# Linear attention with 32 heads (third attention of a layered model): in each step, the first half of the key and value products stands ahead of the weighted products of the step before

## The chip, the cores and the metric

One core of one Trainium2 chip runs the whole program: four layers, each with an attention part and a feed-forward part, and a gating part in front of each. The metric is the device time of one execution in microseconds, as the median of several. Inside the core five engines run on queues of their own and meet only at semaphores: TensorE (PE in the profile, its weight loads PEld), VectorE (DVE), ScalarE (ACT), GpSimd (POOL) and SyncE (SP, which issues the transfers).

## The reference, cut to what matters

The change lies in the attention of the third layer, a linear attention: the keys and values of a head are first contracted over the positions to one 64 by 64 matrix, and the queries are multiplied with that.

```python
B, S, QD = (2, 512, 256)
H, D = (32, 64)
q = jax.nn.relu(proj(Wq))
k = jax.nn.relu(proj(Wk))
v = proj(Wv)
kv = jnp.einsum('bhsd,bhse->bhde', k, v)
qkv = jnp.einsum('bhsd,bhde->bhse', q, kv)
key_sum = k.sum(axis=2)
normalizer = jnp.einsum('bhsd,bhd->bhs', q, key_sum)
normalizer = jnp.clip(normalizer, 1e-06, None)[..., None]
out = qkv / normalizer
...
return out @ Wo + bo
```

The result is added to the running sum x of the model. The gating parts need two recurrences over time for each of eight pieces (256 features by 1024 positions, cut into pieces of 128 by 256), which do not depend on x; those of the three parts that follow are computed inside this attention, in the gaps of the other engines.

## The kernel before

`stage_l2_attn` (L1708) takes the 32 heads as 16 pairs and the 1024 positions as two sequences of 512, so 32 steps: step n handles pair n // 2 and sequence n % 2. The code counts them as j = 0 to 3 within i = 0 to 7. Below, a *period* is four steps, j = 0 to 3.

For one step TensorE computes these groups, named here by letters:

- Q(n), `queries` (L1897): 6 matmuls of 512 columns into the one bank ps_q. Operands are split in a high and a low half, so each product is three matmuls.
- K0(n) and K1(n), `keys_values` with h = 0 and 1 (L1907): 12 matmuls of 256 columns each into the halves of ps_kvp, keys and values of 256 positions each.
- C(n), `key_value` (L1916): keys times values over positions, into ps_kv. These are float32 products, which the profile lists as 8 matmuls of 130 columns.
- W(n), `weighted` (L1926): queries times that matrix, the weighted products, into ps_o; also 8 records. It waits for the copy of ps_kv to SBUF (semaphore kv_evac) and for the queries (q_evac).
- T(n), `turn` (L1934): 4 transposes into ps_t, after the division (quot_ready).
- Y0(n) and Y1(n), `output` (L1940): 3 matmuls of 512 columns each, into the one bank ps_y. Each may start only when VectorE has added what stood in ps_y before to xT (semaphore y_added).

The order of TensorE is written out by hand in `step`, and is software-pipelined over three steps: Q(n), W(n-1), K0(n), Y0(n-2), K1(n), T(n-1), Y1(n-2), C(n).

VectorE has an order by hand too. Its step n is: wait for C(n) and copy ps_kv (L1859, two copies, which let W(n) go); the low half of the turned output (L1838); wait for W(n) (semaphore o_done); normalizer, its reciprocal and the division (L1867, L1868, L1870), which let T(n) go; for j = 0 to 2 the recurrences of one gating piece, `piece_scans` (L151, L156, L158: five instructions); the add of Y0(n-1) to xT (L1852, "add 0" here), which lets Y1(n-1) go; for j = 1 to 3 the quotient of a piece, `piece_finish` (L192, L195, L198); the add of Y1(n-1) ("add 1"). VectorE's step n-1 so belongs to the W(n-1) that TensorE computes within its step n, and its add 0 is that of Y0(n-2), for which Y1(n-2) waits in the same TensorE step.

ScalarE moves queries, keys and values from PSUM to SBUF (L1808, L1812, L1813), rounds the turned output to its high half (L1827) and splits weights (L1791, L1796). GpSimd makes the low halves of the weights (L1768, L1773) and the sums of the gating pieces (L175, L177, L180). SP loads the weights of a pair into two buffers in turn.

Of the kernel before, what the change touches and what calls it, by code (L numbers as in the profile page):

```python
# [90 lines left out]
def build_program(nc, io):  # L91
# [40 lines left out]
    def need(eng, semaphore, count):  # L132

        if not isinstance(count, int) or count > 0:
            eng.wait_ge(semaphore, count)
# [86 lines left out]
    def unread_products(pe, bank, count):  # L222

        for _ in range(count):
            pe.matmul(bank, ident[:, :], fside[:, 0, 0:HALF], start=True, stop=True)  # L225
# [1482 lines left out]
    def stage_l2_attn(l):  # L1708
# [5 lines left out]
        with ExitStack() as st:  # L1714
# [27 lines left out]
            def half_of(x, h):  # L1742
                return x[:, :, h * HALF:(h + 1) * HALF]
# [6 lines left out]
            @block.sync  # L1750
            def _(sp):
                def load(p, k):
                    need(sp, s["w_lo"], p - 1)
                    sp.dma_start(wqkv[:, k, :, :].rearrange("p a b -> p (a b)"), io["l2_wqkv"][p]).then_inc(s[f"wqkv{k}"], 16)
                    need(sp, s["wo_lo"], p - 1)
                    sp.dma_start(wo[:, k, :], io["l2_wo"][p]).then_inc(s[f"wo{k}"], 16)

                for p in range(PAIRS):
                    load(p, p % 2)
# [128 lines left out]
            @block.tensor  # L1888
            def _(pe):
                products = lambda w, x: ((w[0], x[0]), (w[0], x[1]), (w[1], x[0]))  # L1890
                wqkv2, xin2, wo2, oT2 = (wqkv_hi, wqkv_lo), (xin_hi, xin_lo), (wo_hi, wo_lo), (oT_hi, oT_lo)

                def queries(n, j):
                    need(pe, s["q_evac"], n)
                    for k in range(CH):
                        for m, (w, x) in enumerate(products(wqkv2, xin2)):
                            ins = pe.matmul(ps_q[:, :], w[:, j // 2, k, 0:P], half_of(x, j % 2)[:, k, :],  # L1897
                                            start=(k + m == 0), stop=(k == CH - 1 and m == 2))
                    ins.then_inc(s["q_done"], 1)

                def keys_values(n, j, h):
                    need(pe, s["kvp_evac"], 2 * n - 1 + h)
                    for a in range(2):
                        t = j % 2 * HALF + (2 * h + a) * P
                        for k in range(CH):
                            for m, (w, x) in enumerate(products(wqkv2, xin2)):
                                ins = pe.matmul(ps_kvp[:, h, a, :], x[:, k, t:t + P], w[:, j // 2, k, P:3 * P],  # L1907
                                                start=(k + m == 0), stop=(k == CH - 1 and m == 2))
                    ins.then_inc(s["kvp_done"], 1)

                def key_value(n, j):
                    pe.wait_ge(s["kvp_evac"], 2 * n + 2)
                    need(pe, s["kv_evac"], n)
                    for b in range(2):
                        for t in range(2):
                            ins = pe.matmul(ps_kv[:, 2 * HS * b:2 * HS * (b + 1)], ks[:, j % 2, 2 * b + t, :],  # L1916
                                            vs[:, j % 2, 2 * b + t, :, :].rearrange("p r e -> p (r e)"),
                                            start=(t == 0), stop=(t == 1))
                    ins.then_inc(s["kv_done"], 1)

                def weighted(n, j):
                    pe.wait_ge(s["kv_evac"], n + 1)
                    pe.wait_ge(s["q_evac"], n + 1)
                    need(pe, s["quot_ready"], n)
                    for t in range(4):
                        ins = pe.matmul(ps_o[:, t // 2, 2 * HS * (t % 2):2 * HS * (t % 2 + 1)], qT[:, j % 2, t * P:(t + 1) * P],  # L1926
                                        kv[:, j % 2, t // 2, :], start=True, stop=True)
                    ins.then_inc(s["o_done"], 1)

                def turn(n):  # L1930
                    pe.wait_ge(s["quot_ready"], n + 1)
                    need(pe, s["t_low"], n)
                    for t in range(4):
                        ins = pe.transpose(ps_t[:, t * P:(t + 1) * P], quot[:, t, :], ident[:, :])  # L1934
                    ins.then_inc(s["t_done"], 1)

                def output(n, j, ch):
                    need(pe, s["y_added"], 2 * n + ch)
                    for m, (w, o) in enumerate(products(wo2, oT2)):
                        ins = pe.matmul(ps_y[:, :], w[:, j // 2, ch * P:(ch + 1) * P], o[:, j % 2, :],  # L1940
                                        start=(m == 0), stop=(m == 2))
                    ins.then_inc(s["y_done"], 1)

                def step(n, j, i):
                    if j % 2 == 0:
                        pe.wait_ge(s["w_lo"], 2 * i + j // 2 + 1)
                    if n < 2:
                        pe.wait_ge(s["x_lo"], n + 1)
                    queries(n, j)
                    if n >= 1:  # L1950
                        weighted(n - 1, (j + 3) % 4)
                    keys_values(n, j, 0)
                    if n >= 2:
                        k = (j + 2) % 4
                        if k % 2 == 0:
                            need(pe, s["wo_lo"], 2 * i + 1 if j >= 2 else 2 * i)
                        pe.wait_ge(s["t_low"], n - 1)
                        output(n - 2, k, 0)
                    keys_values(n, j, 1)
                    if n >= 1:  # L1960
                        turn(n - 1)
                    if n >= 2:
                        output(n - 2, (j + 2) % 4, 1)
                    key_value(n, j)

                unread_products(pe, ps_y[:, :], 5)
                for n in range(STEPS):
                    step(n, n % PER, n // PER)
                weighted(STEPS - 1, 3)
                pe.wait_ge(s["wo_lo"], PAIRS)  # L1970
                pe.wait_ge(s["t_low"], STEPS - 1)
                for ch in range(CH):
                    output(STEPS - 2, 2, ch)
                turn(STEPS - 1)
                pe.wait_ge(s["t_low"], STEPS)
                for ch in range(CH):
                    output(STEPS - 1, 3, ch)
# [337 lines left out]
```

## Time and profile before

| | |
|---|---|
| median of 3 runs | 1365.04 us (1362.86 to 1367.04) |
| the profiled execution, its own time | 1363.57 us |
| its span | 1361.8 us |
| granted TensorE clock, mean over the span | 0.974 of full |
| PE busy | 1183.8 us, 87% |
| DVE busy | 974.4 us, 72% |
| ACT busy | 611.5 us, 45% |
| POOL busy | 534.5 us, 39% |

All times below are microseconds from the start of the span. 1.77 us of the profiled execution lie outside its span. The attention of the third layer runs from about 826.6 (its first Q) to about 1114. A line of the timeline gives start, duration, engine, line of the kernel, operation, output and inputs, shapes and count; in brackets stands how long the engine was idle before it and what released it. Durations of TensorE's matmuls overlap, so what one group costs is read from the start of its first matmul to the start of the next group's first.

### The profile page before, as it was taken

To read this page: it belongs to the slowest core of one execution; us is meant where nothing else is said; L and a number is where in the kernel's file an instruction comes from. 1 tells how busy PE (TensorE), PEld (TensorE's weight loads), DVE (VectorE), ACT (ScalarE), POOL (GpSimd) and SP (SyncE) were. 2 spreads that over 40 slices of the span, in tenths; PEclk is the share of its full clock that TensorE was granted. 3 is DMA by queue.
4 is the path that set the end of the run, shared out by engine and by line. 5 is a ranking of instruction groups with operands and counts; after the bars stand their busy time and mean duration, and the time that the engine had idled before them with its cause. 6 is when DMAs were issued, how large, how long until landed. Compare 5 with 4: busy or idle time off the path is not lost. (4 is left out here: it accounts for less than half of the span.)

```text
span 1361.8 us, 16948 instructions
## 1 busy us (share of the span) xinstructions
PE 1183.8 (87%) x5900; PEld 833.1 (61%) x5900; DVE 974.4 (72%) x1977; ACT 611.5 (45%) x1423; POOL 534.5 (39%) x440
## 2 busy tenths in 40 slices
PE   0088899999988888999899988999999979399997
PEld 0045556556557766433488866888888853168876
DVE  7969878788768996963633436888888878964355
ACT  2147666666555544445154424333333326143343
POOL 4427866676512221530073323444444420306520
PEclk9999999999999999999799989999999989699999
DMA  2032122121111101400543421111111000011101
GB/s 94 12 80 55 46 55 55 48 54 25 32 33 43 44 20 39 151 0 0 199 153 146 173 75 59 32 32 32 32 32 31 5 8 32 0 48 47 47 28 62
DMA packets 31092, 73.42 MB, mean 54 GB/s; under 512 B 5362, under 2 KB 15091, under 8 KB 28192
## 3 DMA queue, kind: packets, MB, share of 16 engines
q1 hardware_dynamic: 28432, 67.44, 16.2%
q0 software_dynamic: 1536, 3.86, 0.9%
q8 instruction: 47, 0.77, 0.2%
q10 hardware_dynamic: 1040, 1.05, 0.2%
q14 instruction: 37, 0.30, 0.1%
HBM read 55.89 MB, written 6.29 MB: 46 GB/s over the span
## 5 line engine op out<-in xcount | busy, mean ns | idle before, releaser
L175 POOL TENSOR_TENSOR sums<-scans 128x512 f32<-128x512 f32 x64 | 88.1, 1377 | 308.1 <-ACT terms L169 168.4
L727 PE MATMUL ps_p<-xin,wkvq 128*128 128x512 f32 x148 | 74.2, 626 | 68.6 <-DVE xin L243 65.2
L536 ACT ACTIVATE probs<-ps_s,stats 128x256 f32<-128x256 f32 (+1 forms) x256 | 104.3, 419 | 62.1 <-DVE stats L626 60.7
L483 POOL TENSOR_TENSOR probs<-probs,stats 128x512 f32<-128x512 f32 x64 | 67.3, 1051 | 119.1 <-DVE stats L632 119.1
L195 DVE RECIPROCAL sums<-sums 128x256 f32<-128x256 f32 x64 | 112.1, 1752 | 2.0
L626 DVE CUSTOM_DVE_ANT_0 ps_s<-ps_s,mask 128x256 f32<-128x256 f32 (+1 forms) x256 | 82.8, 383 | 8.9 <-PE ps_s L751 8.7
L180 POOL TENSOR_TENSOR sums<-sums,terms 128x512 f32<-128x512 f32 x64 | 84.9, 1326 | 5.0
L727 PEld LDWEIGHTS ps_p<-xin,wkvq 128*128 128x128 f32 x148 | 26.1, 196 | 90.0 <-issue 84.7
L1907 PE MATMUL K_ps_kvp<-K_wqkv_hi,K_xin_hi 128*128 128x256 f32 x256 | 74.7, 292 | 0.0
L1812 ACT ACTIVATE K_ks<-K_ps_kvp 128x256 f32<-128x256 f32 x64 | 24.6, 385 | 109.6 <-PE K_ps_kvp L1907 109.6
L925 POOL TENSOR_TENSOR L3hid<-L3hid,L3sig 128x1024 f32<-128x1024 f32 x17 | 46.1, 2716 | 70.3 <-DVE L3hid L1051 37.8
L1907 PE MATMUL K_ps_kvp<-K_wqkv_lo,K_xin_hi 128*128 128x256 f32 x256 | 72.2, 282 | 0.0
L1907 PE MATMUL K_ps_kvp<-K_wqkv_hi,K_xin_lo 128*128 128x256 f32 x256 | 72.2, 282 | 0.0
L484 POOL TENSOR_TENSOR probs<-probs,stats 128x256 f32<-128x256 f32 x64 | 68.7, 1073 | 0.0
L777 PEld LDWEIGHTS ps_o<-probT,vtok 128*64 128x64 f32 x512 | 31.4, 136 | 52.2 <-issue 29.6
L1051 DVE TENSOR_TENSOR L3hid<-L3actg,L3ps_u 128x512 f32<-128x512 f32 x34 | 23.3, 687 | 54.4 <-ACT L3actg L973 54.4
L751 PE MATMUL ps_s<-kr,qr 64*128 64x256 f32 (+1 forms) x512 | 58.8, 349 | 3.6 <-DVE qr L596 3.4
L777 PE MATMUL ps_o<-probT,vtok 128*64 128x256 f32 (+1 forms) x512 | 55.7, 338 | 3.6 <-ACT oT L551 3.6
L1662 PE MATMUL E_ps<-E_dT,E_fc 128*128 128x256 f32 x256 | 56.6, 379 | 0.6 <-ACT E_dT L1488 0.6
L1676 PE MATMUL E_ps<-E_fc,E_hid 128*128 128x256 f32 x256 | 56.4, 379 | 0.0
L751 PEld LDWEIGHTS ps_s<-kr,qr 64*128 64x128 f32 x512 | 44.0, 186 | 19.9 <-issue 10.5
L1852 DVE TENSOR_TENSOR xT<-xT,K_ps_y 128x512 f32<-128x512 f32 x64 | 43.1, 673 | 17.9 <-PE K_ps_y L1940 17.9
(411 smaller groups left out, 3501.0 us busy)
## 6 DMA issues: line engine op xcount, KB each, us to landing
E_fc<-l_fc_dram SPq DMA_DIRECT2D x16, 1024.0 KB, 7.4
qswap<-qraw SPq DMA_DIRECT2D x60, 128.0 KB, 2.3
K_wqkv<-l_wqkv_dram SPq DMA_DIRECT2D x16, 384.0 KB, 3.2
L3wgu<-L_w_dram SPq DMA_DIRECT2D x17, 256.0 KB, 2.6
L0wgu<-L_w_dram SPq DMA_DIRECT2D x14, 256.0 KB, 2.6
L3wdn<-L_w_dram SPq DMA_DIRECT2D x17, 128.0 KB, 2.0
wkvq<-w_l0a_dram SPq DMA_DIRECT2D x4, 512.0 KB, 4.1
wo<-w_l0a_dram SPq DMA_DIRECT2D x4, 512.0 KB, 3.6
```

Source lines behind the costliest of these rows:

```text
L175: pstep.mark(pool.tensor_tensor(sums[:, k, :, :], scans[:, k, :, 0, :], scans[:, k, :, 1, :], ALU.add))
L180: pool.tensor_tensor(sums[:, k, :, :], sums[:, k, :, :], terms[:, k, :, :], ALU.add).then_inc(sums_ready, 1)
L195: dstep.mark(dve.reciprocal(den, den))
L483: pool.tensor_tensor(p1, p1, rs[:, 0:2].unsqueeze(2).to_broadcast([P, 2, T]), ALU.mult)
L484: pool.tensor_tensor(p0, p0, rs[:, 2:4].unsqueeze(2).to_broadcast([P, 2, P]), ALU.mult).then_inc(s["norm_done"], 1)
L536: ins = act.activation(dst[:, i % 2, :], src[:, i % 2, :], ACT.Exp, bias=stats[:, g % 4, 4 + i:5 + i], scale=-1.0, accum_out=stats[:, g % ...
L626: ins = dve.tensor_tensor_reduce(out=view, in0=view, in1=m, scale=-1.0, scalar=-NEG, op0=ALU.add, op1=ALU.min, accum_out=stats[:, g % 4, 4 ...
L727: ins = pe.matmul(ps[:, :], w[:, k, :], xin[:, k, h * HALF:(h + 1) * HALF], start=(k == 0), stop=(k == CH - 1))
L751: ins = pe.matmul(view[:, r, :], qr[h, (4 * c + m) % 2, b * T + tile * P:b * T + tile * P + P], kr[h, c % 2, b, 0:n], start=True, stop=True)
L777: ins = pe.matmul(o, vtok[:, c % 2, 2 * b + key, 64 * r:64 * r + 64], probT[:, g % 2, r, 0:256] if key == 0 else probT[:, g % 2, r, 256:38 ...
L1662: ins = pe.matmul(ps[:, h, i * CAP:(i + 1) * CAP], fc1[:, k, c, f:f + P], dT[:, c, e * CAP:(e + 1) * CAP], start=(c == 0), stop=(c == CH - 1))
L1907: ins = pe.matmul(ps_kvp[:, h, a, :], x[:, k, t:t + P], w[:, j // 2, k, P:3 * P], start=(k + m == 0), stop=(k == CH - 1 and m == 2))
```

## The change

In TensorE's step the call of K0(n) is moved ahead of W(n-1). Nothing is added or removed. For n = 0 nothing changes, since there is no W before it, and the W of the last step stands behind the loop in both versions.

```diff
                     if n < 2:
                         pe.wait_ge(s["x_lo"], n + 1)
                     queries(n, j)
+                    keys_values(n, j, 0)
                     if n >= 1:
                         weighted(n - 1, (j + 3) % 4)
-                    keys_values(n, j, 0)
                     if n >= 2:
```

## Rows read from the trace of the kernel before

**Rows 1.** The page's first section: busy time and share of each engine.
```profile
PE 1183.8 (87%) x5900; PEld 833.1 (61%) x5900; DVE 974.4 (72%) x1977; ACT 611.5 (45%) x1423; POOL 534.5 (39%) x440
```
**Rows 2.** Busy time of PE, PEld, DVE, ACT, POOL, granted clock, transfers in a window.
```profile
930.00:965.00 35.00, 32.99 (x228) 29.49 (x227) 29.28 (x57) 12.61 (x31) 14.92 (x13) 1.00 0.10 31
```
**Rows 3.** Waits, 827 to 1115: who waited for whom; total us, times, longest.
```profile
DVE K_norm L1867 <- PE K_ps_o L1926: 22.9, 32, 1.6
PEld K_ps_y L1940 <- DVE xT L1852: 18.5, 25, 1.6
...
PEld K_ps_o L1926 <- DVE K_kv L1859: 14.2, 16, 2.0
...
PE K_ps_o L1926 <- DVE K_kv L1859: 7.5, 16, 1.8
```
**Rows 4.** Timeline of PE, two steps with recurrences and the W's that follow.
```profile
936.08 0.48 PE L1897 MATMUL K_ps_q<-K_xin_hi,K_wqkv_hi 128*128 128x512 f32 x1
...
937.55 1.05 PE L1926 MATMUL K_ps_o<-K_kv,K_qT 128*128 128x130 f32 x8
...
938.36 0.36 PE L1907 MATMUL K_ps_kvp<-K_wqkv_hi,K_xin_hi 128*128 128x256 f32 x1
...
939.87 0.40 PE L1940 MATMUL K_ps_y<-K_oT_hi,K_wo_hi 128*128 128x512 f32 x1
...
940.57 0.28 PE L1907 MATMUL K_ps_kvp<-K_wqkv_hi,K_xin_hi 128*128 128x256 f32 x1
...
942.00 0.60 PE L1934 MATMUL K_ps_t<-ident,K_quot 128*128 128x128 f32 x4
943.01 0.50 PE L1940 MATMUL K_ps_y<-K_oT_hi,K_wo_hi 128*128 128x512 f32 x1 [0.41 <-DVE xT L1852]
...
943.80 1.06 PE L1916 MATMUL K_ps_kv<-K_vs,K_ks 128*128 128x130 f32 x8
944.62 0.48 PE L1897 MATMUL K_ps_q<-K_xin_hi,K_wqkv_hi 128*128 128x512 f32 x1
...
946.09 1.05 PE L1926 MATMUL K_ps_o<-K_kv,K_qT 128*128 128x130 f32 x8
...
955.19 1.16 PE L1926 MATMUL K_ps_o<-K_kv,K_qT 128*128 128x130 f32 x8 [0.38 <-DVE K_kv L1859]
...
964.40 1.16 PE L1926 MATMUL K_ps_o<-K_kv,K_qT 128*128 128x130 f32 x8 [0.35 <-DVE K_kv L1859]
```
**Rows 5.** Timeline of PE, the step whose W is followed by no recurrences.
```profile
929.58 1.16 PE L1926 MATMUL K_ps_o<-K_kv,K_qT 128*128 128x130 f32 x8 [0.39 <-DVE K_kv L1859]
...
934.13 0.60 PE L1934 MATMUL K_ps_t<-ident,K_quot 128*128 128x128 f32 x4
934.49 0.48 PE L1940 MATMUL K_ps_y<-K_oT_hi,K_wo_hi 128*128 128x512 f32 x1
```
**Rows 6.** Timeline of DVE: normalizer, division and add 0 of a step; copies.
```profile
938.64 0.17 DVE L1867 TENSOR_SCALAR K_norm<-K_ps_o 128x8 f32<-128x8 f32 x1 [0.78 <-PE K_ps_o L1926]
...
939.08 0.69 DVE L1870 TENSOR_TENSOR K_quot<-K_ps_o,K_norm 128x512 f32<-128x512 f32 x1
...
942.29 0.66 DVE L1852 TENSOR_TENSOR xT<-xT,K_ps_y 128x512 f32<-128x512 f32 x1
...
954.55 0.59 DVE L1859 COPY K_kv<-K_ps_kv 64x130 f32<-64x130 f32 x2
```
**Rows 7.** Timeline of PE: W of steps 0, 1, 2 and 30.
```profile
834.23 1.05 PE L1926 MATMUL K_ps_o<-K_kv,K_qT 128*128 128x130 f32 x8
...
841.29 1.05 PE L1926 MATMUL K_ps_o<-K_kv,K_qT 128*128 128x130 f32 x8
...
850.69 1.16 PE L1926 MATMUL K_ps_o<-K_kv,K_qT 128*128 128x130 f32 x8 [0.29 <-DVE K_kv L1859]
...
1094.55 1.16 PE L1926 MATMUL K_ps_o<-K_kv,K_qT 128*128 128x130 f32 x8 [0.39 <-DVE K_kv L1859]
```
**Rows 8.** Timeline of PE: two 512-column matmuls after some two us of idle.
```profile
410.54 0.47 PE L1109 MATMUL L0ps_g<-L0xin_hi,L0wgu_hi 128*128 128x512 f32 x1 [2.15 <-DVE L0hid L1051]
...
1110.37 0.79 PE L1940 MATMUL K_ps_y<-K_oT_hi,K_wo_hi 128*128 128x512 f32 x1 [2.25 <-DVE K_oT_lo L1838]
```

## The prediction, made before the changed kernel was run

> **What bounds the kernel now.** I read the page's busy shares first: TensorE leads with 87% and VectorE follows with 72% [rows 1]. Then the window of one period inside the stage: in 35 us TensorE is busy 32.99 and VectorE 29.28, at full clock [rows 2]. Two engines near their limit that hand work to each other many times in a step call for the waits and their order, not for shares. The list of waits shows two on TensorE: W for VectorE's copies of ps_kv (16 times) and Y1 for add 0 (25 times), and on VectorE one for W in all 32 steps, 22.9 us [rows 3]. The PE and PEld lines of one wait are the same wait seen by two queues, so they must not be added.
>
> The timeline then gives the loop that matters. The step beginning at Q = 936.08 goes W 937.55, K0 938.36, Y0 939.87, K1 940.57, T 942.00, Y1 943.01, C 943.80, next Q 944.62, next W 946.09 [rows 4]. Costs by differences: Q 1.47, W 0.81, K0 1.51, Y0 0.70, K1 1.43, T 0.36 (934.13 to 934.49, where Y1 does not wait [rows 5]), Y1 0.79, C 0.82. They sum to 7.89. From W to W it takes 8.54, and the difference, 0.65, is the wait of Y1: it could start at 942.36 and starts at 943.01.
>
> Who ends that wait: W starts at 937.55, VectorE's normalizer at 938.64 (+1.09), and after division and five recurrence instructions add 0 runs from 942.29 to 942.95, and Y1 starts 0.06 later [rows 4, 6]. So from W to Y1 there is a chain of 5.46 through VectorE: 1.09 + 3.65 + 0.66 + 0.06. Everything that TensorE has between W and Y1 (0.81 + 1.51 + 0.70 + 1.43 + 0.36 = 4.81) hides under it. This holds for j = 0, 1, 2, whose W is followed by recurrences. For j = 3 there are none, and Y1 does not wait: 929.58 to 937.55 is 7.97 [rows 4, 5].
>
> Two of the four intervals are longer still: 946.09 to 955.19 is 9.10 and 955.19 to 964.40 is 9.21 [rows 4]. There VectorE also has a quotient to finish before the copies (954.55 + 0.59 = 955.14 [rows 6]), and W waits for these. A period is 8.54 + 9.10 + 9.21 + 7.97 = 34.82.
>
> **The change, part by part.** Only K0 moves, from behind W to ahead of it. It issues 12 matmuls and one semaphore increment, and no transfer; it passes no queue but TensorE's.
>
> *What it removes.* With K0 between Q and W, W comes 1.43 later (K1's spacing from 940.57 to 942.00, which is K0's without the slow start behind W). The copies are done 9.05 after the W before (946.09 to 955.14), so W no longer waits. That wait costs (9.10 - 8.54) + (9.21 - 8.54) = 1.23 a period, about 10 us over eight.
>
> *What it adds.* The chain from W to Y1 is not shortened: VectorE cannot begin the normalizer before W has run, and the recurrences stand behind that in its queue, add 0 behind them. But TensorE now has only W, Y0, K1 and T between W and Y1: 0.81 + 0.78 + 1.43 + 0.36 = 3.38 (Y0 taking over the slow start behind W). So Y1 waits 5.46 - 3.38 = 2.08 where it waited 0.65. And K0 has gone into the part of the loop that nothing hides. From W to W: 5.46 + Y1 0.79 + C 0.82 + Q 1.47 + K0 1.43 = 9.97. Behind the waiting Y1 stand C, the next Q, K0 and W; for W waits VectorE, whose idle ahead of the normalizer grows. That is a closed loop, so it repeats in each step with recurrences.
>
> *The four intervals after.* j = 0: 9.97 for 8.54, +1.43. j = 1: 9.97 for 9.10, +0.87. j = 2: 9.97 for 9.21, +0.76. j = 3: VectorE has no recurrences, its add 0 follows the division (2.14 after W by 939.08 + 0.61 against 937.55, or 1.8 by Y0, whichever is later), well ahead of 3.38; so TensorE's own 7.89 holds for 7.97, -0.08. Sum: 37.80 for 34.82, +2.98 a period.
>
> *What I cost at nothing.* ScalarE takes keys and values of K0 earlier relative to W; it idles before each such copy now, and C is 6.25 behind W in the slow steps, so nobody waits. T needs the division, which ends at 2.22 after W (939.08 + 0.69), and T comes at 3.02: cover 0.8, and were it gone, T would only use up part of the wait of Y1. The low halves for Y0 follow the copies (955.14 plus about 0.7), before the new W at 9.97 after the old. GpSimd's work and SP's loads get more time, not less.
>
> *The sum.* W(0), at 834.23, comes 1.43 later, and W(1) with it. W(1) to W(2) I take as another j = 1, +0.87. From W(2) at 850.69 to W(30) at 1094.55 are seven periods (243.86 us [rows 7]), 7 x 2.98 = 20.9. Behind W(30) the loop ends: the last W has no Q and K0 ahead of it, and its chain is as before. Together 1.43 + 0.87 + 20.9 = 23.2. On the profiled execution's own time, 1363.6, that is 1386.8; on the median, which lies 1.5 above it, 1388.2. I take the middle, 1387.5.
>
> *Bounds.* The uncertain term is 5.46. For the third W it may be some 0.15 more, since that W itself took 0.1 longer (1.16 against 1.05 [rows 4]), and it may shrink as little if VectorE's work meets GpSimd's elsewhere. 0.15 in 22 loops is 3.3 us; a run moves by 2. This gives 1382 to 1393.
>
> *The clock.* Idle of TensorE grows to about 1.8 us (2.08 less the tail of T) in three steps of four. After 2.15 us of idle a 512-column matmul at 410.54 still took 0.47, full speed; after 2.25 us at the end of this stage, where other waits had come just before, one took 0.79 for 0.50 [rows 4, 8], which is the lower of the two levels, 1.2 for 2.4 GHz. So the rows allow both, and the steady stage stands at 1.00 [rows 2]. The Trainium skill, page "TensorE: Matmul & The Clock Gate", section "A second HAM failure mode: psum-queue depth-cycling", says that short idles between groups of matmuls, repeated each iteration, can be enough to make the clock swing between its levels. By that rule the change would cost more than my sum; of the trace, only the row at 1110.37 speaks for it.
>
> **The rivals.** *Slower by the clock:* if one loop of each period ran at half clock from Y1 to W, its 0.79 + 0.82 + 1.47 + 1.43 = 4.51 would double: 8 x 4.5 = 36 more, 1423.
>
> *Faster:* W's wait goes and Y1's does not grow. It would need a chain from W to Y1 of at most 5.46 - 1.43 = 4.03. Then the gain is the 10 us above: 1354. For it speaks only that W's wait stands in the list; against it that 3.65 of the chain are VectorE instructions in a fixed queue.
>
> *No change:* VectorE is the bound in all steps, and a later W only moves the wait from W to Y1, one for one: 1364. This decides if VectorE has no idle between steps. It has, 22.9 us ahead of the normalizer, so it follows W.
>
> *Half of it:* only the j = 0 loops lengthen (8 x 1.43 = 11.4), because the quotients hide the rest: 1375. It needs copies later than 9.97 behind W; they are at 9.05.
>
> **How the numbers follow.** Forecast 0.80, clock 0.07, half 0.05, faster 0.04, no change 0.04. The range 1375 to 1395 takes in the bounds, a little on both sides for a mis-sized term, and the half case: over 0.8. A measurement of this kernel tells about 0.3% from no change, 4 us. Faster 0.04, same 0.04, slower 0.92.
>
> **What would show it.** The wait of W for the copies gone from the list of waits; that of Y1 for add 0 three times as long (about 24 x 2 us, less the overlap); W to W 9.97, 9.97, 9.97, 7.89; the normalizer's wait for W grown; clock 1.00. I am wrong if add 0 comes less than 4 us after W, if W to W stays near 9.1, or if matmuls of 512 columns in the stage take 0.79.

## The result, and the profile after

The changed kernel takes 1396.42 us in the median of four runs (1391.54 to 1398.08), the kernel before 1365.29 in the same comparison: a ratio of 1.0225, with an interval of 1.0199 to 1.0251, 31 us slower. The sign was forecast, the size (23 us) was not reached, and the time lies 1.4 us above the stated range. The profiled execution of the changed kernel took 1391.54, with a span of 1389.8, 28.0 longer than before.

The page's first section and the waits of the stage, from the changed kernel:

```profile
PE 1184.6 (85%) x5900; PEld 839.1 (60%) x5900; DVE 985.1 (71%) x1977; ACT 611.0 (44%) x1423; POOL 536.0 (39%) x440
```

```profile
PEld K_ps_y L1940 <- DVE xT L1852: 50.7, 25, 2.1
DVE K_norm L1867 <- PE K_ps_o L1926: 47.9, 32, 3.4
...
PEld K_ps_o L1926 <- DVE K_kv L1859: 2.7, 1, 2.7
```

Beside [rows 3]: the wait of W for the copies is gone but for the one in the last step (16 times before, once now). The wait of Y1 for add 0 has grown from 18.5 to 50.7 us, still 25 times, and VectorE's own wait for W from 22.9 to 47.9. TensorE's work is the same as in [rows 1] within 1 us; of the 28.0 us of span 27.2 are its idle time. VectorE is busy 10.7 us longer with the same 1977 instructions; the experiments trace that to one of them.

The timeline of TensorE through one step with recurrences (start, duration, engine, line, operation, count, idle before and what ended it) shows the loop:

```profile
950.94 1.05 PE L1926 MATMUL K_ps_o<-K_kv,K_qT 128*128 128x130 f32 x8
951.75 0.48 PE L1940 MATMUL K_ps_y<-K_oT_hi,K_wo_hi 128*128 128x512 f32 x1
...
953.96 0.60 PE L1934 MATMUL K_ps_t<-ident,K_quot 128*128 128x128 f32 x4
956.39 0.50 PE L1940 MATMUL K_ps_y<-K_oT_hi,K_wo_hi 128*128 128x512 f32 x1 [1.83 <-DVE xT L1852]
...
957.18 1.06 PE L1916 MATMUL K_ps_kv<-K_vs,K_ks 128*128 128x130 f32 x8
958.00 0.48 PE L1897 MATMUL K_ps_q<-K_xin_hi,K_wqkv_hi 128*128 128x512 f32 x1
...
960.90 1.05 PE L1926 MATMUL K_ps_o<-K_kv,K_qT 128*128 128x130 f32 x8
```

W at 950.94, Y1 at 956.39: the chain is 5.45 (5.46 before [rows 4]). T begins at +3.02, and Y1 is then held for 2.07 from where it could start. From W to W it is 9.96. VectorE in the same step:

```profile
952.03 0.17 DVE L1867 TENSOR_SCALAR K_norm<-K_ps_o 128x8 f32<-128x8 f32 x1 [1.86 <-PE K_ps_o L1926]
...
955.68 0.66 DVE L1852 TENSOR_TENSOR xT<-xT,K_ps_y 128x512 f32<-128x512 f32 x1
...
958.28 0.60 DVE L1859 COPY K_kv<-K_ps_kv 64x130 f32<-64x130 f32 x2 [0.21 <-PE K_ps_kv L1916]
...
961.99 0.17 DVE L1867 TENSOR_SCALAR K_norm<-K_ps_o 128x8 f32<-128x8 f32 x1 [2.39 <-PE K_ps_o L1926]
```

The normalizer comes 1.09 after W and add 0 starts 3.65 after that, as in [rows 6]. The copies are done at 958.88, and the W for which they were to be early comes at 960.90. In j = 1 and 2, where a quotient stands ahead of them, they are done 9.75 us behind W. VectorE idles 2.39 before it can go on.

Reading the start of each W in the same way gives the whole stage. The table holds the intervals of a typical period and the time from W(0) to W(31), which is free of what happens before and behind the loop. An interval is named by the j of the step whose W opens it; the first, W(0) to W(1), and the last, W(30) to W(31), are apart from the pattern, and of the 29 between them 22 belong to steps with recurrences. These are the "22 loops" below:

| | W to W, j = 0, 1, 2, 3 | W(0) to W(31) |
|---|---|---|
| before | 8.54, 9.11, 9.21, 7.97 | 269.5 |
| changed | 9.96, 9.97, 9.96, 7.88 | 296.0 |
| forecast | 9.97, 9.97, 9.97, 7.89 | 269.5 + 21.8 |

Of the 31 intervals 26 lie within 0.03 of 9.97 or 7.89. Three are 11.56 to 11.58 instead of 9.96: 3 x 1.6 = 4.8 us. The first is unchanged (7.05), and the last is 9.80 for 9.20, because this W waited for copies that stood behind the long max (L192) that the experiments show below; W(1) to W(2), forecast as 9.40 + 0.87, came out 9.98, which makes up half of that. The sum: 28.0 in the span = 1.5 by which W(0) itself is later, + 26.5 in the loop; without the three long intervals 23.2 is left, the figure that was forecast. That it agrees to the tenth is luck: the last interval's 0.6 more, which was not forecast, is made up by W(1) to W(2) and by seven periods that together grew 20.5 and not 20.9. From W(31) to the end of the span both kernels take 258.05.

One of the long intervals:

```profile
873.64 0.60 PE L1934 MATMUL K_ps_t<-ident,K_quot 128*128 128x128 f32 x4
876.08 0.50 PE L1940 MATMUL K_ps_y<-K_oT_hi,K_wo_hi 128*128 128x512 f32 x1 [1.84 <-DVE xT L1852]
...
876.89 1.62 PE L1916 MATMUL K_ps_kv<-K_vs,K_ks 128*128 128x130 f32 x8
878.16 0.78 PE L1897 MATMUL K_ps_q<-K_xin_hi,K_wqkv_hi 128*128 128x512 f32 x1
878.74 0.63 PE L1897 MATMUL K_ps_q<-K_xin_lo,K_wqkv_hi 128*128 128x512 f32 x1
...
882.20 1.05 PE L1926 MATMUL K_ps_o<-K_kv,K_qT 128*128 128x130 f32 x8
```

and the windows around it, whose last columns are the granted clock, the transfers' share and GB/s:

```profile
872.00:882.00 10.00, 8.16 (x46) 7.21 (x45) 5.94 (x12) 2.04 (x5) 3.23 (x3) 0.83 0.13 42
882.00:892.00 10.00, 8.16 (x58) 7.40 (x58) 8.53 (x16) 3.74 (x9) 4.76 (x4) 1.00 0.01 2
```

Y1 still runs at full speed here after 1.84 us of idle (in another of the three, at 897.61, it already took 0.75). Then C takes 1.27 from its start to Q's instead of 0.82, and the matmuls of Q are 0.43 apart instead of 0.23: the lower of the two levels, 1.2 for 2.4 GHz. K0 is at full speed again. The granted clock of this window is 0.83, that of a neighbour without such a stretch, with the same share of busy time (8.16 of 10 us), is 1.00. In the kernel before it is 1.00 in [rows 2], and 1.00 in the mean of 827 to 1103, where its last W comes; the fall at 1110.37 [rows 8] lies behind that.

### The profile page after: what moved, and what is told of

It is laid out like the page before. It is cut to its first block and busy times, and to the rows that moved or that the text cites. A ratio compares the mean times of both kernels' runs of the same rounds, so it can differ in the third digit from the quotient of the medians.

```text
span 1389.8 us, 16948 instructions
## 1 busy us (share of the span) xinstructions
PE 1184.6 (85%) x5900; PEld 839.1 (60%) x5900; DVE 985.1 (71%) x1977; ACT 611.0 (44%) x1423; POOL 536.0 (39%) x440
## 3 DMA queue, kind: packets, MB, share of 16 engines
q10 hardware_dynamic: 1040, 1.05, 0.2%
## 5 line engine op out<-in xcount | busy, mean ns | idle before, releaser
L1940 PE MATMUL K_ps_y<-K_oT_hi,K_wo_hi 128*128 128x512 f32 x64 | 32.3, 504 | 45.3 <-DVE xT L1852 43.9
L1808 ACT ACTIVATE K_qT<-K_ps_q 128x512 f32<-128x512 f32 x32 | 19.2, 599 | 100.4 <-PE K_ps_q L1897 100.4
```

## The experiments

Each was timed against the kernel before on its own chip (1364.1 to 1364.9 there). Five questions: is the rest above 23 us the clock; is the chain through add 0 the loop; does the price follow the amount moved; what was missing when it did not; and does VectorE's order allow a faster kernel.

**The changed kernel again.**

> The changed kernel once more, beside the others on one chip. My theory: the order alone costs 23 us (a loop from W to W of 9.97 us in steps with recurrences), and what is above that, 5 us in the profile and about 8 in the median, is TensorE's clock falling to its lower level after some of the 2.08 us waits of Y1, 1.6 us each time. Expected again 1391 to 1398 us, with some W to W intervals of 11.6 us and a window clock of about 0.83 there, the others at 9.97. The rival, that the extra is not tied to these waits, expects the long intervals elsewhere too, in steps where Y1 does not wait (7.89).

1396.43 us (1392.29 to 1406.82), ratio 1.0259 (1.0219 to 1.0298). Its profiled execution has two long intervals, 11.56 each, both in steps with recurrences; the others are 9.95 to 9.99 and 7.86 to 7.88. W(0) to W(31) is 294.4, less 2 x 1.6 it is 291.2. The long intervals do not lie in the same steps as in the first profile. A third fall in it, behind a Y1 at 1127.52, cost nothing, since the last W waited for its copies anyway (the interval is 9.81). And W(0) comes 10.58 behind the first Q, where in the first profile it came 9.09: there matmuls of Q at 827.44 to 828.68 ran at the lower level. That is at the entry of the stage and not in the loop.

**The wait filled with matmuls.** The edit, in the changed kernel:

```diff
                     if n >= 2:
+                        if j > 0:
+                            pe.wait_ge(s["q_evac"], n + 1)
+                            for _ in range(12):
+                                pe.matmul(ps_q[:, 0:256], xin_hi[:, 0, 0:P], xin_hi[:, 1, 0:256], start=True, stop=True)
                         output(n - 2, (j + 2) % 4, 1)
```

> The changed kernel with 12 matmuls of 256 columns, whose result nobody reads, ahead of each Y1 that waits (into ps_q, already evacuated). They take 1.43 us of a wait of 2.08, so TensorE is idle 0.65 there as in the kernel before, while the loop from W to W through VectorE stays 9.97. If the idle costs the clock: no interval of 11.6, clock 1.00 in the stage, time 1365.3 + 23.2 = 1388.5, some 5 to 8 below the changed kernel. If the clock falls for another reason: the time of the changed kernel, 1392 to 1398, and long intervals left. If TensorE's own work were the bound and not the chain through VectorE: 22 x 1.43 = 31 us slower than the changed kernel.

1388.98 us (1387.41 to 1391.15), ratio 1.0181 (1.0164 to 1.0198), where 1388.5 was expected. More work, 7.4 us less time than the changed kernel. Two of the three stretches in which the changed kernel had a clock of 0.83, here (the third, 912 to 922, is at 1.00 as well):

```profile
872.00:882.00 10.00, 9.59 (x71) 8.87 (x71) 6.21 (x13) 2.75 (x8) 3.27 (x3) 1.00 0.19 54
892.00:902.00 10.00, 9.60 (x72) 8.88 (x70) 9.20 (x16) 2.75 (x8) 3.56 (x4) 1.00 0.18 54
```

No interval is longer than 9.97, and W(0) to W(31) is 291.1. The 22 loops remain at 9.96 although TensorE has 1.43 more to do in each, so TensorE's work is not what paces them, and the idle, 1.84 in the changed kernel and 0.41 here, is what lowers the clock. So 24 of the 31 us are the order and 7 the clock. At 1.6 us each 7.4 us would be four or five long intervals in the median run, against three and two in the profiled ones; that number is an estimate from the medians, since the other runs have no trace. Their mean granted clocks point the same way: 0.964 to 0.968 in seven of the eight runs of the changed kernel, 0.970 to 0.975 in the four of this one. The eighth run of the changed kernel, 1406.82, had 0.956; if all of its 14.5 us above the profiled 1392.29 are such stretches, they are nine more.

**Half of the move.** `keys_values` takes a list of its two parts; the first stands ahead of W and the second behind.

```diff
-                    keys_values(n, j, 0)
+                    keys_values(n, j, 0, (0,))
                     if n >= 1:
                         weighted(n - 1, (j + 3) % 4)
+                    keys_values(n, j, 0, (1,))
```

> Only the first 6 of K0's 12 matmuls stand ahead of W, the other 6 behind it. My loop: 5.46 + 0.79 + 0.82 + 1.47 + 0.71 = 9.25 from W to W for j = 0, 1, 2, and 7.97 or 7.89 for j = 3, so a period of 35.65 for 34.82: 7 x 0.83 + 0.9 = 6.7 us slower than before, 1372; the wait of Y1 1.37, too short to cost the clock. If the cost were proportional to what is moved (half of 31 us): 1381. If it is a fixed price of the new order: about 1390 or more.

1380.75 us (1379.93 to 1384.39), ratio 1.0117 (1.0100 to 1.0134): a miss by 9, and right where a proportional price would have put it. The intervals say that this is a coincidence. They are 9.25, 9.81, 9.92, 7.96: the first is what the loop gives, and in the next two it is not Y1's loop that ends last but W's wait for the copies, back again at 16 times. VectorE's and GpSimd's timelines show why the copies are late:

```profile
961.68 0.66 DVE L1852 TENSOR_TENSOR xT<-xT,K_ps_y 128x512 f32<-128x512 f32 x1
962.26 1.08 DVE L192 TENSOR_SCALAR sums<-sums 128x256 f32<-128x256 f32 x1
```

```profile
961.91 1.28 POOL L175 TENSOR_TENSOR sums<-scans 128x512 f32<-128x512 f32 x1 [5.92 <-ACT terms L169]
```

The max at L192 takes 1.08 here. The answers for that line over the stage (minimum, median, maximum in ns) in the kernel before, in this one and in the changed one:

```profile
L192 DVE TENSOR_SCALAR sums<-sums x24: 279/284/291, 847.0 to 1106.6; 128x256 f32<-128x256 f32 x24
```

```profile
L192 DVE TENSOR_SCALAR sums<-sums x24: 286/1080/1091, 851.4 to 1127.3; 128x256 f32<-128x256 f32 x24
```

```profile
L192 DVE TENSOR_SCALAR sums<-sums x24: 284/1076/1090, 848.1 to 1134.6; 128x256 f32<-128x256 f32 x24
```

The end of the max shown above, 963.34, lies just behind the end of GpSimd's sum, 963.19. Moving part of K0 let ScalarE deliver its exponential (L169) earlier in the step: 4.89 us behind W, where it was 5.62 in the kernel before. With it GpSimd starts its sum 4.97 behind W and so just before the max, which starts at 5.32; in the kernel before the sum started at 5.69, when the max was over.

**The same, with GpSimd held back.** One wait more for GpSimd, ahead of each piece:

```diff
                         for k in ((0, 1), (2,))[j // 2]:
+                            need(pool, s["y_added"], 2 * (PER * i + k - 1) + 1)
                             piece_pool(pool, l + 1 + k, i, k % 2)
```

> The half-moved kernel, with GpSimd's first sum of a piece (L175) waiting also for add 0. In the half-moved kernel W to W was 9.81 and 9.92 for j = 1 and 2, not 9.25, since VectorE's max (L192) took 1.08 us instead of 0.28: it stood up against GpSimd's sum, which had begun just before. My theory is that this contention is the missing 9 us: with the sum held back until add 0 is done, the max starts first, takes 0.28, W to W is 9.25 for j = 1 and 2 too, and the time is 1372. If the max is long for another reason, its duration stays 1.08 and the time 1381.

1371.48 us (1369.72 to 1374.31), ratio 1.0058 (1.0039 to 1.0078): 9.3 us less, by a wait added (8.7 less if each is taken from the kernel before on its own chip, 15.9 and 7.2 above it). The intervals are 9.25, 9.25, 9.25, 7.87, and the max is short again:

```profile
964.58 0.28 DVE L192 TENSOR_SCALAR sums<-sums 128x256 f32<-128x256 f32 x1
```

```profile
964.74 1.28 POOL L175 TENSOR_TENSOR sums<-scans 128x512 f32<-128x512 f32 x1 [3.23 <-DVE xT L1853]
```

Now VectorE's instruction is first, and GpSimd's starts after it. That shows the contention and its price, and with it gone the price of moving half of K0 is the forecast of the loop, 7 us. In the fully changed kernel the same 0.8 us lie in VectorE's queue too, but there the copies are done 9.75 behind W and W comes at 9.96, so they cost nothing but in the last step. What the two engines contend for, no run shows.

**Add 0 ahead of the recurrences**, in the changed kernel (`add_first`) and in the kernel before (`add_first_before`):

```diff
+                    if earlier:
+                        add(n - 1, j + 1, 0)
                     if j < 3:
                         piece_scans(dve, l + 1 + j, i, j % 2)
-                    if earlier:
-                        add(n - 1, j + 1, 0)
```

> The changed kernel, and on VectorE add 0 stands ahead of the five recurrence instructions instead of behind them. My theory is that these 2.9 us between the division and add 0 make the loop. Then the wait of Y1 is gone (add 0 ends 2.8 after W, Y1 comes at 3.38), j = 0 and j = 3 take TensorE's own 7.9, j = 1 and 2 the 9.1 that VectorE needs from W to the copies: a period of 34.2 for 34.8, and the time is 1362, 34 below the changed kernel and 3 below the kernel before. The rival, that W's lateness costs VectorE itself (its idle ahead of the normalizer) whatever the order of add 0, expects 1385 or more.

1360.18 us (1357.08 to 1362.11), ratio 0.9966 (0.9955 to 0.9977): 36 us below the changed kernel. The wait of Y1 for add 0, 25 times in the others, is there twice:

```profile
DVE K_norm L1867 <- PE K_ps_o L1926: 39.6, 32, 3.0
PEld K_ps_o L1926 <- DVE K_kv L1859: 21.8, 16, 4.0
...
PEld K_ps_y L1940 <- DVE xT L1852: 2.9, 2, 1.5
```

VectorE still waits for W, 39.6 us in all, so that idle by itself is no loss; the rival that made it the cause is out. The intervals are 7.87, 9.02, 9.12, 7.97: the first and the last are TensorE's own work, the two between what VectorE needs from W to the copies.

> The kernel before (K0 behind W), with add 0 ahead of the recurrences. If my chain is right, here the same edit on VectorE hurts: Y0 comes 2.32 after W, so add 0 can start only about 3.3 after it, VectorE idles 1.1 between the division and add 0, and W to W is 8.0, 10.2, 10.3, 8.0: a period of 36.5 for 34.8, time 1377. So with this VectorE order the move of K0 that cost 31 us is worth 17 us (1360 against 1377). If the recurrences ahead of add 0 are all that matters, it is faster than the kernel before, 1358 to 1361.

1387.47 us (1386.75 to 1390.89), ratio 1.0178 (1.0159 to 1.0198). The same edit, which takes 36 us off the changed kernel, puts 23 on the kernel before; and with this order on VectorE the move of K0 is worth 27 us. The intervals are 7.86, 10.10, 10.21, 7.98, close to the forecast, but six of the eight third ones are 11.73 to 11.78: there W waits long for the copies, and the clock falls.

```profile
961.10 1.40 PE L1926 MATMUL K_ps_o<-K_kv,K_qT 128*128 128x130 f32 x8 [2.07 <-DVE K_kv L1859]
...
964.86 0.60 PE L1940 MATMUL K_ps_y<-K_oT_hi,K_wo_hi 128*128 128x512 f32 x1
```

W takes 1.40 for 1.05, and from W to Y0 it is 3.76 for 2.32. Six times 1.5 us are 9, and the forecast of 1377 is 10 too low: the clock was left out again, in a kernel with a wait of 2 us. That is not the whole account. The period without the long intervals is 36.15 and not 36.5, about 2.5 us less over the stage, and behind W(31) the rest of the kernel takes 4.0 us longer than in the kernel before (262.1 for 258.05), which was not forecast; there W(31) itself, after 3.45 us of idle, and the outputs behind it run at the lower level.

**The copies ahead of the quotient.** In the changed kernel, VectorE's order becomes division, add 0, recurrences, the copies of the next step, add 1, quotient (`copies_early`); the max moved ahead of add 0 as well (`copies_early_max`). The edit of `copies_early`, shortened, against `add_first`; the two copies become a function of their own:

```diff
                     if j < 3:
                         piece_scans(dve, l + 1 + j, i, j % 2)
+                    if n + 1 < STEPS:
+                        copies(n + 1, j + 1)
+                    if earlier:
+                        add(n - 1, j + 1, 1)
                     if j > 0:
                         piece_finish(dve, l + j, i, (j - 1) % 2)
-                    if earlier:
-                        add(n - 1, j + 1, 1)
```

> The changed kernel; VectorE: division, add 0, recurrences, copies of the next step, add 1, quotient. The copies no longer stand behind the quotient, so W does not wait for it, and VectorE works through TensorE's W. VectorE's work is 8.9 us in j = 1 and 2, 6.4 and 6.0 in j = 0 and 3, 30.3 a period; TensorE's is 31.5. Expected: a period of about 32.8 (VectorE is late for T in j = 2 and 3 by some 1.3 us), time 1351, below both kernels. If VectorE's lateness does not get made up, 1360 as with add 0 first alone. Contention of the max with GpSimd can add up to 0.8 in two steps of a period, 1363.

1374.34 us (1370.96 to 1376.72), ratio 1.0070 (1.0047 to 1.0093). A miss by 23, and slower than with add 0 first alone.

> As copies_early, and the max of the quotient (L192) stands ahead of add 0, where GpSimd is less often at work. Expected 1348 to 1351 if the max was long in copies_early, otherwise no better (the max is then 0.3 us more ahead of add 0, for which Y1 waits only from 3.38 on).

1365.26 us (1361.29 to 1366.09), ratio 1.0003 (0.9993 to 1.0012). Better by 9, so the position of the max mattered (its median falls from 0.58 us to 0.28), but 14 to 17 us above what was expected. Both misses show one thing in VectorE's timeline (a wait of 2.70 in the second); here that of `copies_early` in j = 3:

```profile
970.54 0.69 DVE L1852 TENSOR_TENSOR xT<-xT,K_ps_y 128x512 f32<-128x512 f32 x1
974.01 0.59 DVE L1859 COPY K_kv<-K_ps_kv 64x130 f32<-64x130 f32 x2 [2.77 <-PE K_ps_kv L1921]
974.63 0.69 DVE L1852 TENSOR_TENSOR xT<-xT,K_ps_y 128x512 f32<-128x512 f32 x1
975.24 0.69 DVE L192 TENSOR_SCALAR sums<-sums 128x256 f32<-128x256 f32 x1
975.96 1.75 DVE L195 RECIPROCAL sums<-sums 128x256 f32<-128x256 f32 x1
```

In the step without recurrences VectorE stands 2.77 us at the copies, waiting for C, while its quotient, which it could do, is queued behind them; that quotient then delays the next step's division. I had counted VectorE's work and not where it has to wait.

**The quotient ahead of the copies in j = 3 only.** The edit, shortened, against `copies_early_max`:

```diff
+                    if j == 3:
+                        piece_quotient(dve, l + j, i, (j - 1) % 2, 1)
+                        piece_quotient(dve, l + j, i, (j - 1) % 2, 2)
                     if n + 1 < STEPS:
                         copies(n + 1, j + 1)
                     if earlier:
                         add(n - 1, j + 1, 1)
-                    if j > 0:
+                    if j in (1, 2):
```

> As copies_early_max, but in j = 3, which has no recurrences, the reciprocal and the product of the quotient stand ahead of the copies again. With the copies ahead, VectorE idled 2.7 us in j = 3 waiting for C, with its quotient still to do, and W to W was 7.86, 9.25, 8.82, 8.55. My theory is that VectorE's queue order in j = 3, not its load, was lost there: now j = 3 takes 7.9, the period is 33.8, the time 1358. If VectorE is simply overloaded, the period stays 34.5 and the time 1365.

1359.76 us (1356.48 to 1362.18), ratio 0.9969 (0.9958 to 0.9979). The intervals are 7.87, 9.24, 8.83, 7.88, a period of 33.8 as expected. In this list and in that of the expectation the order is j = 1, 2, 3, 0, by the W that opens each: what shrank, from 8.55 to 7.88, is the interval behind the step without recurrences, where the late division was paid, while the one of j = 3 stays 8.83. W(0) to W(31) is 258.9, 10.6 less than before, of which the median keeps 4: behind the last W its VectorE still has a quotient of the step before to do, TensorE idles 2.54 and goes on at the lower level, and the next stage's first matmul comes 15.1 after W(31), where it came 11.7 after it.

**Add 0 first, once more.**

> The changed kernel with add 0 ahead of the recurrences once more, in more rounds, since its gain is small: 1360 against 1364.5 for the kernel before, ratio 0.9966, with an interval clear of 1. Intervals from W to W 7.87, 9.02, 9.12, 7.97.

1361.48 us (1358.02 to 1363.54), ratio 0.9977 (0.9965 to 0.9989). The gain over the kernel before is 3 to 5 us in the two comparisons, and clear of none in both. The changed kernel with two calls exchanged on VectorE is faster than the kernel before and the changed one; `copies_mixed` does so by about the same (4.4 us).

## Why the prediction was wrong

*Who paces the stage: right.* The chain from W through the division and the recurrences to add 0 and Y1 was put at 5.46 and stayed at 5.45 in the changed kernel, in the filled and in the half-moved one. `add_first` shows that it is the cause: take the recurrences out of it, and the loss is gone.

*What is removed: right.* The wait of W for the copies disappeared.

*What is added: right.* Three intervals of 9.97 and one of 7.89 were forecast, 9.96, 9.97, 9.96 and 7.88 came, and the half-moved kernel without contention gave 9.25 as its sum says. The order alone costs 23.2 us in the profile (forecast 23.2, the last tenths by luck), and 24 in the median by the filled kernel.

*What I cost at nothing: right for this kernel, by 0.2 us.* GpSimd's work was said to get more time. It also came earlier in VectorE's step, and this made one VectorE instruction four times as long, 0.8 us in two steps of a period. With W at 9.96 and the copies done at 9.75 the cover was enough but in the last step (0.6); with W at 9.25 it was not, and it cost 9 us. I had not looked at whether the instructions that would now stand side by side can run side by side.

*The clock: wrong, and this is the step that failed.* I worked out an idle of 1.8 us in three steps of four, read that a matmul after 2.15 us of idle was still at full speed and one after 2.25 was not [rows 8], and put the fall at a chance of 0.07, as an extra of 36 us or nothing, outside the range. It fell, but in a few of the 22 loops and for 1.6 us each: 4.8 us in the profiled execution, about 7 in the median. Two things were wrong in that step. The row at 410.54 was given the greater weight, though it is a single idle and not one in each step; nor does the first matmul behind an idle tell whether the clock falls, since in the changed kernel the one at 876.08 took 0.50, full speed, and C, 0.81 later, did not. The clock had even been at the lower level shortly before that row, in 402.3 to 405.6 (a granted clock of 0.74 in 400 to 405) with no idle of more than 1.05 us in the ten before, so the length of an idle was not all that there was to read. And the rival was sized as a whole period's loss at once, while part of it, a few us, belonged in the upper end of the range of the forecast itself: 1388.2 on the median + 7 is 1395, against an upper end of 1395 and a measured 1396.4.

The profile shows the fall right behind a repeated idle of 1.84 us. The Trainium skill, page "TensorE: Matmul & The Clock Gate", section "A second HAM failure mode: psum-queue depth-cycling", was quoted against the change for this; the trace agrees with it, with 7 us as the price. Another sentence of that page, in "Why this matters for your kernels", warns only of idles longer than these; here 1.84 us was enough at times, so the measurement decides against taking shorter ones as safe.

## What to carry to other kernels

Before moving work ahead of a waiting instruction, find the chain that hangs on the instruction that is made to wait. If it comes back to the same queue, everything moved ahead of it leaves the part that the chain hides and joins the part that nothing hides, and the loop gets longer by its full length, even though the wait that one saw does vanish. Then ask of the chain's other engine which of its instructions can be exchanged: the same move cost 31 us with one order of two calls there and gained about 27 with the other.

## What the runs showed that was not expected

TensorE's clock fell after idles of 1.8 to 2.1 us that recur each step or once a period, in two or three of 22 loops in one kernel and in six of eight periods in another. It never fell in the loop where the idle before Y1 was 0.41 (before, filled) or 1.12 (half-moved). Each fall cost 1.5 to 1.6 us here. Why it came in some loops and not in others with the same idle, the runs do not show.

VectorE's max of one SBUF tile of 128x256 took 0.28 us when it began before GpSimd's sum and 1.08 when it began 0.35 after it, ending just behind it; delaying GpSimd by a wait made the kernel 9 us faster. In `copies_early` the max and GpSimd's product (L177) begin within 0.02 of each other in j = 2, and either may lose: at 859.56 the max took 0.90 and the product 0.75, at 966.33 the max took 0.29 and the product 0.90. The interval behind the first kind is 9.5, behind the second 8.9. The Trainium skill, page "SBUF — State Buffer", section "Who interferes with whom", says that the two engines share a pair of ports, that an instruction like this maximum (a tensor_scalar) can take it, and that whoever issues first holds it for the whole instruction while the other blocks. The trace agrees: 1.08 for 0.28 where GpSimd was first, and 0.90 for 0.75 on GpSimd in the second of these two steps. Where the max began 0.16 ahead of the sum, GpSimd's 1.28 show no delay.
